# Order of ScalarE's and TensorE's work at the seam between step parts and feature stages of a two-layer graph attention kernel

## The reference

```python
h = jnp.maximum(_layernorm(x, axis=-1), 0.0)
x = x + _L0_gnn_ref(h, adj, L0_gnn_W, L0_gnn_a_src, L0_gnn_a_dst)
h = jnp.maximum(_layernorm(x, axis=-1), 0.0)
x = x + _L1_gnn_ref(h, adj, L1_gnn_W, L1_gnn_b, L1_gnn_a)
# a layer: f = h @ W.T (+ b); s_src, s_dst = f @ a_src, f @ a_dst
#   e = leaky_relu(s_src[i] + s_dst[j], 0.2), masked where adj is 0
#   out = softmax(e, over j) @ f
```

## Time and profile before

| | |
|---|---|
| median of 3 runs | 2893.46 us (2893.43 to 2896.14) |
| the profiled execution | 2893.4 us |
| its span, first to last instruction | 2891.3 us |
| PE busy | 2507.4 us (87%) |
| DVE busy | 2008.3 us (69%) |
| ACT busy | 1631.4 us (56%) |
| POOL busy | 1367.9 us (47%) |
| mean granted TensorE clock | 0.944 |

### The profile page before, as it was taken

The page is one execution under the profiler, slowest core; times in us unless marked ns, Lnnn a source line. Parts: engine busy times, 40 slices in busy tenths (PEclk is TensorE's granted clock), DMA queues, the critical chain, the costliest instruction groups (busy, mean ns, idle before and its releaser), DMA issues. The chain is left out here.

```text
span 2891.3 us, 56693 instructions
## 1 busy us (share of the span) xinstructions
PE 2507.4 (87%) x22166; PEld 2256.3 (78%) x22166; DVE 2008.3 (69%) x3326; ACT 1631.4 (56%) x3058; POOL 1367.9 (47%) x1757
## 2 busy tenths in 40 slices
PE   4986999979998899979999699997999979996686
PEld 3875888768887788858888588885888868885686
DVE  1557776686667676776776777768777587766996
ACT  4026665565555655656556555566556565653564
POOL 2113554545544345553555444453555535544566
PEclk9998999989999899989999899998999989998898
DMA  7641333223342134322433213341343223200010
GB/s 130 75 52 29 60 68 57 40 37 63 64 54 50 30 64 66 45 48 36 65 63 45 54 31 68 64 64 29 61 68 56 41 38 56 49 16 23 16 42 19
DMA packets 197737, 147.26 MB, mean 51 GB/s; under 512 B 143072, under 2 KB 144224, under 8 KB 197472
## 3 DMA queue, kind: packets, MB, share of 16 engines
q1 hardware_dynamic: 179040, 110.07, 16.0%
q0 software_dynamic: 18432, 33.56, 14.0%
HBM read 193.60 MB, written 50.66 MB: 84 GB/s over the span
## 5 line engine op out<-in xcount | busy, mean ns | idle before, releaser
L649 ACT ACTIVATE shared<-Rb,w 128x512 int8<-128x512 f32 x1728 | 1083.7, 721 | 362.0 <-DVE shared L1092 358.5
L821 PE MATMUL accA<-S,shared 128*128 128x257 f32 x4096 | 975.9, 391 | 75.0 <-DVE shared L1027 71.4
L840 PE MATMUL accB<-Sw,shared 128*128 128x195 bf16 x7680 | 977.3, 250 | 70.9 <-DVE shared L1096 65.2
L821 PEld LDWEIGHTS accA<-S,shared 128*128 128x128 f32 x4096 | 772.8, 194 | 184.8 <-DVE shared L1027 83.4
L846 PE MATMUL accB<-Sv,shared 128*128 128x130 f16 x7680 | 764.1, 223 | 0.0
L840 PEld LDWEIGHTS accB<-Sw,shared 128*128 128x128 fp8e4 x7680 | 640.7, 98 | 121.7 <-issue 83.1
L1027 DVE SCALAR_TENSOR_TENSOR shared<-Rb,w,mask 128x512 f32<-128x512 f32 x512 | 421.8, 838 | 387.3 <-PE accA L821 341.5
L846 PEld LDWEIGHTS accB<-Sv,shared 128*128 128x128 fp8e4 x7680 | 577.8, 99 | 0.9
L468 POOL TENSOR_SCALAR shared<-shared 128x260 f32<-128x260 f32 x128 | 130.3, 1018 | 721.9 <-ACT shared L691 721.8
L1092 DVE TENSOR_TENSOR shared<-shared,mask 128x512 uint32<-128x512 uint32 x432 | 329.0, 762 | 191.6 <-ACT shared L649 149.0
L1096 DVE TENSOR_TENSOR shared<-shared,mask 128x512 uint32<-128x512 uint32 x512 | 396.7, 775 | 8.9
(11 more groups left out here) (103 smaller groups left out, 2393.9 us busy)
## 6 DMA issues: line engine op xcount, KB each, us to landing
Rb<-R_dram SPq DMA_DIRECT2D x160, 256.0 KB, 3.5
adj_bytes<-in_adj POOLq DMA_DIRECT2D x128, 256.0 KB, 5.3
xb<-in_x SPq DMA_DIRECT2D x32, 512.0 KB, 3.9
out<-xb SPq DMA_DIRECT2D x32, 512.0 KB, 2.8
mask<-adj_bytes SPq DMA_TRANSPOSE x128, 4.4
shared<-in_W SPq DMA_DIRECT2D x2, 256.0 KB, 2.9
R_dram<-R_rows SPq DMA_DIRECT2D x8, 32.0 KB, 1.8
a_cols<-in_a SPq DMA_DIRECT2D x8, 0.2 KB, 11.4
```

Of the source, the lines that this page charges most:

```text
L649: last = nc.scalar.activation(cmp[:, slot, jj // 2, of_pair(jj % 2, 0, CI)], Rb[:, h, :], ACT.Sign, bias=w[1][:, JG * g + jj, h:h + 1], sc ...
L821: last = nc.tensor.matmul(accA[:, k, 0:F + 1], tiles[:, j % RING, k * P:(k + 1) * P], S0[:, j, 0:F + 1], start=j == 0, stop=j == NJ - 1)
L840: nc.tensor.matmul(acc[:, bank, col:col + NS], bits[:, g % BRING, 1, jj // 2, of_pair(jj % 2, k * P, P)], Sw[:, j, h, :, :].rearrange("p a ...
```

## The change

Three edits.

1. Layer 1's normalization of chunk 1 moves on ScalarE from the feature stage, where it stood behind `move_yt(1, 0)`, into the step part of the phase before, right behind chunk 0's at the last "X1" event. Its wait on `x1_ready` moves with it, with the same meaning (phase ph + 1 there is ph in `features`). In an AB phase this is ahead of the last head's EB copy; in phase 0 no EB follows. The number of instructions is the same.
2. `turn_rows(1)` on TensorE and `move_rows(1)` on ScalarE come at t = 2 in the loop over layer 0's chunks, not at t = 1.
3. `low(0)` and `low(1)` on ScalarE come behind the whole loop, ahead of `exps(0)`.

```diff
                 if kind != "A":
                     move_yt(1, 0)
-
-                    wait(act, S["x1_ready"], NC * ph + 1)
-                    norm(ph, 1, 1)
                     for t in range(1, NC):
                         move_yt(1, t)
...
                     if t + 1 < NC:
                         move_yt(0, t + 1)
-                    if both and t == 1:
+                    if both and t == 2:
                         move_rows(kind, ph, 1)
...
                     move_features(t, [2, 3])
-                    if both and t >= 2:
-                        low(t - 2)
+                if both:
+                    for t in range(NC - 2):
+                        low(t)
                 exps(0)
...
                             act.wait_ge(S["n_ready"], HG * (n - NC) + (NR + HG))
                         norm(ph + 1, 1, 0)
+
+                        act.wait_ge(S["x1_ready"], NC * (ph + 1) + 1)
+                        norm(ph + 1, 1, 1)
...
                     if t + 1 < NC:
                         turn_y(0, t + 1)
-                    if both and t == 1:
+                    if both and t == 2:
                         turn_rows(1)
```

## The result

The changed kernel takes **2874.2 us** (median of 4 runs, 2867.9 to 2875.7); the kernel before, run beside it, 2894.8 (2893.4 to 2896.1). The ratio is 0.9925, 95% interval 0.9908 to 0.9942. So 20.5 us are saved, where 6.5 were forecast. The profiled execution of after is 2875.2 us with a span of 2873.0, 18.3 less than before's. Over all comparisons the kernel before ran from 2884.1 to 2898.4 us; single executions differ by several microseconds, and so I compare stage by stage as well.

A forecast was written before the change was run, and what follows sets the result against it. TensorE bounds the step parts; each feature stage chains TensorE's layer 1, a short reduction, VectorE's 31 us and row factors through HBM. 2893.4 - 8.6 + 0.3 + 1.8 = 2886.9 us, range 2881 to 2893.

The forecast's parts named there:

- the one on the clock: Half-clock stretches of TensorE stay otherwise as they are; three more or fewer called ordinary, 4.5 us either way.
- the case that all six go: Layer 1 features: all six stages lose their half-clock stretch, 6 x 1.6 = 9.7 us more, 2877.2 us; chance 0.04.
- The rival: Ahead of layer 1, less TensorE idle spares half-clock stretches: 2881 to 2884 us, or 2877.2 for all six; chance 0.22.
- a price of 0.77 us: Layer 1's second transposes on TensorE take 1.04 us like the first instead of 1.81, 0.77 us earlier.
- The direct saving: Stages 2 to 8: layer 1's features start 1.23 us earlier in each, 7 x 1.23 = 8.6 us saved.
- 0.3 for the statistics: VectorE's layer 0 chunk 2 statistics wait for GpSimd's factor of chunk 0; 0.3 us charged in all, bounds 0 and 1.5.
- Stage 1's loss: Stage 1: yT's move stands behind the wait for the update; 1.8 us lost, with a 3.41 us half-clock stretch; lower bound 0.
- the 0.2 us named as next in line: Chunk 2's statistics wait 0.2 us for GpSimd's result, only where layer 1 runs as fast as in stage 2.
- Parts 2 and 3: Later row factors and low halves work beneath VectorE's 31 us; worth 0, TensorE's wait growing to about 12 us.
- (c): End of layer 1: VectorE, GpSimd or a slipped sums' copy stops the gain; 2892 to 2895 us, chance 0.10.
- (d): Step parts: half-clock stretches go from 13 to 28, 20.6 us slower, 2907 us; chance 0.05.

The follow-up runs named there:

- the 4 added transposes: The kernel before, with 4 identity transposes in TensorE's 2.3 us idle ahead of layer 1's chunk 1 transposes, slow transposes kept: 2893.6 us, ratio 1.0003.
- the filled run: The kernel before, with 12 unused identity transposes between TensorE's transposes of chunks 0 and 1 in stages 1 to 8: 2868.5 us, ratio 0.9912.
- part 1 alone: The kernel before with only chunk 1's normalization moved ahead of the last sums' copy, the other two edits undone: 2876.7 us, ratio 0.9938.
- two copies: The changed kernel with two more 128x256 copies on ScalarE ahead of the move of yT, results unused: 2890.2 us, ratio 0.9995.
- parts 2 and 3 alone: The kernel before with row factors turned a chunk later and low halves behind all layer 0 copies, normalization not moved: 2893.2 us, ratio 0.9999.
- keep1: The changed kernel, but with ScalarE's old order at the seam of phases 0 and 1: 2865.5 us, ratio 0.9907.
- one copy: The changed kernel with one more 128x256 copy on ScalarE ahead of the move of yT, result unused: 2875.5 us, ratio 0.9944.
- fill_steps: keep1 with 12 identity transposes ahead of head 0's first masks' matmuls in each step-part chunk but the first: 2847.8 us, ratio 0.9850.
- the last kernel: fill_steps with 20 more identity transposes in TensorE's 6 us wait for the first tile of each step part: 2846.7 us, ratio 0.9842.

## Why the prediction was wrong

**The step that failed is the one on the clock.** The sum ended "with the number of half-clock stretches otherwise as it is", and the argument for it was that 1.83 us of idle is near to 2.32. I gave the case that all six go 0.04, with 2877.2 us. It is what happened, while the step parts kept their 13. The rival named the "gaps in the slower transposes" in passing, but the comparison that set its chance left them out: the transposes behind the idle are spread over 1.81 us instead of 1.04. The run with the 4 added transposes shows that this spreading, with an idle of 1.88 us, is enough for a stretch in every stage; the filled run prices the stretches at 9.3 us in all. I had 1.6 each, measured 1.5. The size of the term was known, its sign and count were guessed, and the second transposes' own length was given a price of 0.77 us but no weight in the count. No row of the kernel before could have settled the count by itself: its stage 2 had the same idle and spread, and no stretch.

**The direct saving was right.** Forecast 7 x 1.23 = 8.6 less 0.3 for the statistics, 8.3; shown 8.8, as the difference between the filled kernel and the changed one. The normalization followed the update by 0.14 us (539.22 to 539.36; forecast 0.15) and the copy was not late. TensorE followed yT's move within 0.05 us, where I took 0.17 from another pair, so the features start 3.71 us after the first transpose and not 3.8. In stage 2 the statistics of chunk 2 wait for GpSimd:

```profile
553.76 1.40 DVE L881 BATCH_NORM_STATS2 stats<-xb 128x6 f32<-128x256 f32 x4 [0.15 <-POOL shift L409]
```

that is the 0.2 us named as next in line, and stage 2 gained 1.04 us where the others gained 1.3.

**Stage 1's loss was right, its size in part by luck.** Forecast 1.8 us, measured 1.94. TensorE idles 4.86 us and then runs at half clock:

```profile
190.32 1.82 PE L734 MATMUL accA<-ident,shared 128*128 128x128 f32 x8 [1.69 <-ACT shared L540]
197.00 1.97 PE L734 MATMUL accA<-ident,shared 128*128 128x128 f32 x8 [4.86 <-ACT shared L550]
198.76 4.90 PE L748 MATMUL accA<-WT,shared 128*128 128x264 f32 x16
```

But the stretch is not the one of 3.41 us behind TensorE's start that the sum used. It lasts 6.83 us, from 194.31 to 201.14, and begins within the idle; 4.14 us of it lie over transposes and features. The windows of its two pieces:

```profile
194.31:197.00 2.69, 0.00 (x0) 0.00 (x1) 2.52 (x11) 2.64 (x8) 0.96 (x3) 0.50 0.00 0
197.00:201.14 4.14, 4.14 (x14) 3.62 (x15) 2.42 (x13) 2.13 (x6) 3.52 (x9) 0.50 0.00 0
```

The kernel before has a stretch in stage 1 too, and there it costs nothing, which bears out that VectorE's statistics set the pace. Its window, and that of the filled kernel, which has none:

```profile
190.44:216.25 25.81, 21.67 (x103) 16.69 (x104) 18.05 (x65) 14.40 (x35) 8.48 (x20) 0.93 0.00 1
190.75:216.57 25.82, 22.04 (x115) 17.09 (x116) 18.06 (x64) 14.34 (x35) 8.48 (x20) 1.00 0.00 1
```

**Parts 2 and 3 were worth 0**, as the run of them alone shows, and VectorE's 31.03 us stayed. Rivals (c) and (d) did not come.

**What was not in the sum.** The way from layer 0's maximum to the first tile in stage 1 was 2.7 us longer in before's profile than in after's. It is a slow store of the row factors, 2.97 us from the store's issue to the load's, where 1.35 to 1.40 is usual, and a load behind it that landed 4.2 us after its issue and not 3.1. A store of layer 0's row factors this slow (3.0 to 3.4 us) came once in each of four of the ten kernels profiled up to the last (before, part 1 alone, the two copies, the 4 transposes) and never in the others. It came with part 1 and without it, so I do not put it down to the change. It inflates the difference of the two profiled spans; how often it falls in the executions that were not profiled is not known.

**What stays open** is the number of stretches in the step parts of kernels whose step parts are equal. Their length goes by it: 273.7 to 275.2 us with none, 275.5 to 276.6 with one, 277.0 to 278.7 with two, 279.1 and 279.2 with three. It also goes by how long TensorE stays at half clock from the first tile on, 3.6 to 7.0 us. A fit over the 63 parts of these nine kernels gives 1.5 us for each stretch and 0.5 for each us more at the start, and is off by 0.3 us at most; it is an estimate. Before had 13 stretches in the profiled run, after 13, part 1 alone 13, parts 2 and 3 alone 12, the filled kernel 8, keep1 8, one copy 10, two copies 13, the 4 transposes 12. The wait at which they lie is the same in all. By the fit, five stretches fewer are 7.5 us, most of why keep1 gained 8.7 us where 2 were due; that the count is also behind the spread between executions fits their granted clocks (keep1's run of 2873.7 us has 0.948, its others 0.950 and 0.951), but those were not profiled. What decides which of the equal waits is followed by a stretch was not settled; in one kernel, shortening the wait removed them all.

## What to carry to other kernels

Where TensorE's work is dense behind a short wait, price the wait twice: its length, and the half-clock stretch that may follow it, which here was worth as much (9.3 us and 8.8). Look at the granted clock of each stage and at how tightly the matmuls around a wait are packed; a few matmuls whose result nobody uses, put into the wait, tell in one run what the clock costs, and may stay as the remedy (fill_steps, part 1 with such matmuls in the step parts: 2847.8 us against 2892.9, the kernel to keep). A step moved into another engine's idle time must be followed to the variants of the seam that have no such idle time: stage 1 paid 1.9 us that leaving it alone gave back.

## What the runs showed of the hardware that I had not expected

An idle of TensorE of 1.9 to 2.7 us is enough for a half-clock stretch of 3.41 us at its end, but not reliably: with tight matmuls around it none of seven stages at 1.74 us, two at 2.05 and five at 2.35; with 1.88 us and spread transposes, seven. Equal waits in the step parts had one at 13 of the 21 places in one kernel and at 8 in another. The idle of 4.86 us had one of 6.83 us, which began before it ended.

Transposes of the identity keep the full clock: 12 of them, 1.47 us, removed the stretches of layer 1's features and of the step parts. Behind a long wait at half clock, 20 of them brought the full clock early in two of seven places only.

A 128x256 copy on ScalarE put ahead of other work delayed it by 0.31 us, where four in a row of the same size (L540) take 2.08.

In the three slow stores of row factors in stage 1 and in the one of stage 6, an instruction fetch of 0.02 MB fell into the same 8 us of DMA traffic; in stage 1 of seven other traces, none did:

```profile
q8 instruction: 1, 0.02, 0.4%
```

(the queue's line of the DMA view in before, 250 to 266 us; columns: packets, MB, share). By the packets' start times it is closer than that. The eleven traces hold 176 stores of row factors. Behind seven of them a fetch starts within 0.1 to 1.0 us of the store's issue, and these are the seven slow ones: layer 0's take 2.17 us (the last kernel, stage 4) and 2.97 to 3.39 us in place of 1.4, layer 1's 2.33 and 2.58 in place of 1.8. None of the other 169 is slow. Whether the fetch delays the store was not tried.
